# Cross-attention scores in three rounds of four key tiles, and products with the values of all heads once a batch, in a decoder layer

## The reference

```python
q = proj(hs, Wq, bq, S); k = proj(at, Wk, bk, T); v = proj(at, Wv, bv, T)
scores = jnp.einsum('bhsd,bhtd->bhst', q, k) / scale
scores = jnp.where(attend, jnp.clip(scores, -50.0, 50.0), -10000.0)
probs = jax.nn.softmax(jnp.clip(scores, -50.0, 50.0), axis=-1)
ctx = jnp.einsum('bhst,bhtd->bhsd', probs, v)
delta = rs * (ctx.transpose(0, 2, 1, 3).reshape(B, S, H) @ Wo.T + bo)
```

## Time and profile before

| | |
|---|---|
| runs | 1500.3 us median of 3 (1499.81 to 1503.2) |
| profiled execution | 1502.32 us; its span, first to last instruction, 1500.5 us |
| TensorE busy in the span | 1446.0 us, 96% |
| VectorE, ScalarE, GpSimd busy | 1051.9, 656.6, 579.7 us |
| mean granted TensorE clock | 0.986 |

### The profile page before, as it was taken

The page is one execution under the profiler, slowest core; times in us unless marked ns, Lnnn a source line. Parts: engine busy times, 40 slices in busy tenths (PEclk is TensorE's granted clock), DMA queues, the critical chain, the costliest instruction groups (busy, mean ns, idle before and its releaser), DMA issues. The chain is left out here.

```text
span 1500.5 us, 33618 instructions
## 1 busy us (share of the span) xinstructions
PE 1446.0 (96%) x13322; PEld 1125.9 (75%) x13322; DVE 1051.9 (70%) x2017; ACT 656.6 (44%) x861; POOL 579.7 (39%) x510
## 2 busy tenths in 40 slices
PE   7999999999899999999999999999999995998898
PEld 3688888887788888888888888888888884554333
DVE  2766655564577877777777777777777866677778
ACT  1333333333343433433334334333343432888986
POOL 0000000000244455444545454454545552752566
PEclk9999999999999999999999999999999997999999
DMA  6023333321511112111121121211212112357974
GB/s 217 29 78 102 102 102 101 102 81 45 182 40 61 52 45 72 45 47 64 45 72 44 41 71 45 72 39 45 72 45 70 41 56 64 81 171 285 355 260 154
DMA packets 80406, 138.58 MB, mean 92 GB/s; under 512 B 4882, under 2 KB 52498, under 8 KB 78562
## 3 DMA queue, kind: packets, MB, share of 16 engines
q1 hardware_dynamic: 80354, 137.87, 28.1%
HBM read 93.82 MB, written 44.04 MB: 92 GB/s over the span
## 5 line engine op out<-in xcount | busy, mean ns | idle before, releaser
L737 POOL TENSOR_TENSOR xa_psum<-xa_pr 125x448 f32<-125x448 f32 x126 | 153.9, 1221 | 236.0 <-DVE xa_pr L883 236.0
L883 DVE TENSOR_SCALAR xa_pr<-xa_pr,xa_keep 125x448 f32<-125x448 f32 x384 | 151.0, 450 | 108.1 <-ACT xa_pr L783 106.7
L783 ACT ACTIVATE xa_pr<-xa_bSC 125x1344 f32<-125x1344 f32 x128 | 165.6, 1294 | 138.1 <-PE xa_bSC L989 133.0
L764 ACT ACTIVATE xa_kf<-xa_bKV,xa_bk 128x376 f32<-128x376 f32 x128 | 73.8, 576 | 184.8 <-PE xa_bKV L913 184.8
L740 POOL TENSOR_TENSOR xa_psum<-xa_psum,xa_pr 125x448 f32<-125x448 f32 x126 | 147.3, 1169 | 12.1 <-POOL xa_psum L737 4.4
L913 PE MATMUL xa_bKV<-left_xn,wA 128*128 128x376 f32 x768 | 150.0, 344 | 0.0
L913 PE MATMUL xa_bKV<-xa_cx,wA 128*128 128x376 f32 x768 | 149.3, 343 | 0.0
L770 ACT COPY xa_v<-xa_bKV 125x512 f32<-125x512 f32 x96 | 56.3, 586 | 206.1 <-PE xa_bKV L924 200.9
L924 PE MATMUL xa_bKV<-wZ,left_xn 128*125 128x512 f32 x576 | 141.8, 394 | 1.7 <-POOL xa_ones L713 1.7
L924 PE MATMUL xa_bKV<-wZ,xa_cx 128*125 128x512 f32 x576 | 141.1, 393 | 0.0
L913 PEld LDWEIGHTS xa_bKV<-left_xn,wA 128*128 128x128 f32 x768 | 130.1, 188 | 8.9 <-issue 5.3
(11 more groups left out here) (192 smaller groups left out, 2560.3 us busy)
## 6 DMA issues: line engine op xcount, KB each, us to landing
wraw<-in_ctxT SPq DMA_DIRECT2D x32, 752.0 KB, 4.8
ff_hr<-h_scratch SPq DMA_DIRECT2D x7, 2048.0 KB, 11.1
wraw<-in_w SPq DMA_DIRECT2D x8, 1024.0 KB, 7.6
sa_raw<-in_x SPq DMA_DIRECT2D x8, 896.0 KB, 5.9
x_scratch<-left_qraw SPq DMA_DIRECT2D x8, 896.0 KB, 5.0
xa_qf<-q_scratch SPq DMA_DIRECT2D x32, 224.0 KB, 4.7
xa_x<-x_scratch SPq DMA_DIRECT2D x32, 224.0 KB, 4.7
x_scratch<-xa_x SPq DMA_DIRECT2D x32, 224.0 KB, 2.3
```

Source lines behind the costliest of these rows:

```text
L737: nc.gpsimd.tensor_tensor(psum01[:], third(h, 0), third(h, 1), ALU.add).then_inc(p01_ok, 1)
L764: nc.scalar.activation(kf[:, m, :], bKV[0][:, 0:TP], ACT.Identity, bias=bkt[:, m:m + 1]).then_inc(k_ok, 1)
L783: nc.scalar.activation(pr[h][:], bSC[0:TW, :, 0:TC * S], ACT.Exp, scale=XSCALE).then_inc(exp_ok, 1)
L883: nc.vector.tensor_scalar(third(h, t), third(h, t), EM50, bound, ALU.max, ALU.min).then_inc(pr_ok, 1)
```

## The change

The 12 tiles of scores of a batch (four heads of three) are counted through as units and computed in three rounds of four units (UR, NR), so that head 1 begins in round 0 and ends in round 1, and head 2 begins in round 1 and ends in round 2. pr has three buffers of four tiles in place of four of three, psum one buffer for each head and no psum01. TensorE's order in a batch becomes: scores round 0; attend of all four heads of the batch before, then sums of all four; keys 2, values 0 of the next batch; scores round 1, keys 3, values 1 of the next batch; scores round 2, keys 0 of the next batch, output of the batch before, keys 1 and values 2 of the next batch. The four products of a batch with their sums lie in the two banks bPV at once (pv_bank). tail2 and tail3 move one batch later, and so do the store of x2 and norm2. The last batch has an order of its own. The diff, cut:

```diff
--- before.py
+++ after.py
@@ -36,6 +36,8 @@
+UR = 4
+NR = C * TC // UR
@@ -637,8 +639,8 @@
-        pr = [n.sb(f"pr{i}", [TW, NJ, TC * S]) for i in range(C)]
-        psum01, psum = n.sb("psum01", [TW, NJ, S]), [n.sb(f"psum{i}", [TW, NJ, S]) for i in range(2)]
+        pr = [n.sb(f"pr{i}", [TW, NJ, UR * S]) for i in range(NR)]
+        psum = [n.sb(f"psum{h}", [TW, NJ, S]) for h in range(C)]
@@ -668,8 +670,27 @@
-        def third(h, t):
-            return pr[h][:, :, t * S:(t + 1) * S]
+        def early(b):
+            return isinstance(b, int) and b < 2
+        def tile_of(h, t):
+            u = h * TC + t
+            return pr[u // UR], u % UR * S
+        def part(h, t):
+            own, at_col = tile_of(h, t)
+            return own[:, :, at_col:at_col + S]
+        def units(r):
+            return [divmod(u, TC) for u in range(r * UR, (r + 1) * UR)]
+        def last_head(r):
+            return units(r)[-1][0]
+        def pv_bank(b, h):
+            if last(b):
+                return bPV[h][:, 0:2 * S] if h < 2 else bSC[:, h - 2, 0:2 * S]
+            return bPV[h % 2][:, h // 2 * 2 * S:(h // 2 + 1) * 2 * S]
@@ -692,19 +713,20 @@
-                    wait(sp, sc_done, 4 * b)
+                    wait(sp, sc_done, NR * b)
                     queries(b + 1, 1 - par)
+                if not early(b):
+                    sp.wait_ge(amax_ok, b - 1)
+                    sp.dma_start(x2_d[b - 2], x1[par][:]).then_inc(x2_out[par], 16)
                 wait(sp, x2_out[par], 8 * (b - par))
...
-                if not first(b):
-                    sp.wait_ge(amax_ok, b)
-                    sp.dma_start(x2_d[b - 1], x1[1 - par][:]).then_inc(x2_out[1 - par], 16)
@@ -727,21 +749,32 @@
+            def pair_sum(b, h):
+                pool.wait_ge(pr_ok, C * TC * b + TC * h + 2)
+                wait(pool, sum_done, C * (b - 1) + h + 1)
+                nc.gpsimd.tensor_tensor(psum[h][:], part(h, 0), part(h, 1), ALU.add).then_inc(p01_ok, 1)
+            def full_sum(b, h):
+                pool.wait_ge(pr_ok, C * TC * b + TC * h + 3)
+                pool.wait_ge(p01_ok, C * b + h + 1)
+                nc.gpsimd.tensor_tensor(psum[h][:], psum[h][:], part(h, 2), ALU.add).then_inc(ps_ok, 1)
...
+                if not early(b):
+                    norm2(b - 2)
+                pair_sum(b, 0)
+                full_sum(b, 0)
+                pair_sum(b, 1)
+                full_sum(b, 1)
+                if not first(b):
+                    x1_beta(b - 1, 1 - par)
+                if not last(b):
+                    pair_sum(b, 2)
+                    full_sum(b, 2)
+                    pair_sum(b, 3)
+                    full_sum(b, 3)
+                if not first(b):
+                    norm(b - 1)
@@ -772,25 +805,32 @@
+            keys(0, 1)
...
+            values(0, 0, 2)
+            def weights(b, r):
+                act.wait_ge(sc_done, NR * b + r + 1)
+                wait(act, pv_done, C * (b - 1) + last_head(r) + 1)
+                wait(act, ps_ok, C * (b - 1) + last_head(r) + 1)
+                nc.scalar.activation(pr[r][:], bSC[0:TW, :, 0:UR * S], ACT.Exp, scale=XSCALE).then_inc(exp_ok, 1)
...
+                weights(b, 0)
+                keys(b, 2)
+                if not last(b):
+                    values(b + 1, 1 - par, 0)
+                weights(b, 1)
+                keys(b, 3)
+                if not last(b):
+                    values(b + 1, 1 - par, 1)
+                weights(b, 2)
+                if not last(b):
+                    keys(b + 1, 0)
+                    if not (isinstance(b, int) and b >= B - 2):
...
+                    keys(b + 1, 1)
+                    values(b + 1, 1 - par, 2)
@@ -820,8 +860,8 @@
+                bank = pv_bank(b, h)
+                dve.wait_ge(sum_done, s + 1 if last(b) else C * b + C)
@@ -833,11 +873,11 @@
+            def tail1(b, mv=mv, st=st, bank=bKV[1]):
...
+                nc.vector.tensor_tensor(dl[:], bank[0:S, 0:D], bot[:], ALU.add).then_inc(dl_ok, 1)
@@ -871,35 +911,48 @@
+            def bounded(b, r):
+                dve.wait_ge(exp_ok, NR * b + r + 1)
+                for h, t in units(r):
+                    bound = keep[:, b * TC + t:b * TC + t + 1] if isinstance(b, int) else keep[:, bass.ds(b * TC + t, 1)]
+                    nc.vector.tensor_scalar(part(h, t), part(h, t), EM50, bound, ALU.max, ALU.min).then_inc(pr_ok, 1)
...
+                if not last(b):
+                    split_low(b + 1, 1 - par)
+                if not early(b):
+                    tail2(b - 2, par)
+                bounded(b, 0)
+                if not first(b):
+                    attended(b - 1, 0)
+                    attended(b - 1, 1)
+                if last(b):
+                    attended(b - 1, 2)
+                    attended(b - 1, 3)
+                bounded(b, 1)
+                if not first(b) and not last(b):
+                    attended(b - 1, 2)
+                    attended(b - 1, 3)
+                if not early(b):
+                    tail3(b - 2, par)
+                if first(b):
+                    for c in range(C):
+                        output_weights(c)
+                if last(b):
+                    tail1(b - 1)
+                    attended(b, 0)
+                    bounded(b, 2)
+                    attended(b, 1)
+                    return
+                bounded(b, 2)
+                if not first(b):
+                    tail1(b - 1)
...
+            attended(B - 1, 2)
+            attended(B - 1, 3)
...
+            tail1(B - 1, mv1, st1, bKV[0])
@@ -918,6 +971,7 @@
+                if t == 2:
@@ -926,18 +980,20 @@
+                bank = bKV[0] if last(b) else bKV[1]
+                if first(b):
+                    pe.wait_ge(wo_ok, 2 * C)
+                if last(b):
+                    pe.wait_ge(k_ok, 4 * B)
+                else:
+                    wait(pe, dl_ok, b)
+                    pe.wait_ge(v_ok, 3 * B if isinstance(b, int) and b == B - 2 else 3 * b + 8)
...
+                        mm = nc.tensor.matmul(bank[0:S, 0:D], cT[l][:, c, :], w["o"][r][:, c, :],
@@ -946,76 +1002,85 @@
+            keys(0, 0, 1)
+            values(0, 0, 2)
...
+                bank = pv_bank(b, h)
...
+                    wait(pe, cthi_ok, C * b)
+                pe.wait_ge(pr_ok, C * TC * b + TC * h + 3)
...
+                    own, col = tile_of(h, t)
...
+                bank = pv_bank(b, h)
...
+                        own, col = tile_of(h, t)
...
+                pe.wait_ge(ps_ok, C * b + h + 1)
...
+            def scores(b, par, r):
+                if r == 0:
+                    pe.wait_ge(q_in[par], 8 * (b - par) + 16)
+                pe.wait_ge(k_ok, 4 * b + last_head(r) + 1)
+                wait(pe, exp_ok, NR * b + r)
+                for i, (h, t) in enumerate(units(r)):
+                    for j in range(NJ):
+                        own = slice(j * HD, (j + 1) * HD)
+                        mm = nc.tensor.matmul(bSC[0:TW, j, i * S:(i + 1) * S], kf[own, h, t * TW:(t + 1) * TW], qf[par][own, h, :],
+                                              start=True, stop=True)
+                mm.then_inc(sc_done, 1)
...
+                scores(b, par, 0)
+                if not first(b):
+                    for h in range(C):
+                        attend(b - 1, 1 - par, h)
+                    for h in range(C):
+                        sums(b - 1, h)
+                keys(b, par, 2)
+                if not last(b):
+                    values(b + 1, 1 - par, 0)
+                scores(b, par, 1)
+                keys(b, par, 3)
+                if last(b):
+                    attend(b, par, 0)
+                    sums(b, 0)
+                    output(b - 1)
+                    scores(b, par, 2)
+                    attend(b, par, 1)
+                    sums(b, 1)
+                    return
+                values(b + 1, 1 - par, 1)
+                scores(b, par, 2)
+                keys(b + 1, 1 - par, 0)
+                if not first(b):
+                    output(b - 1)
+                keys(b + 1, 1 - par, 1)
+                values(b + 1, 1 - par, 2)
...
+            attend(B - 1, 1, 2)
+            sums(B - 1, 2)
...
+            attend(B - 1, 1, 3)
+            sums(B - 1, 3)
...

```

More of the change, by code:

```diff
@@ L834, in attended @@
                                                in1=cT[0][:, h, :].bitcast(F32), op0=ALU.add, op1=ALU.subtract).then_inc(ctlo_ok, 1)
-            def tail1(b, mv=mv, st=st):
+            def tail1(b, mv=mv, st=st, bank=bKV[1]):
                 if first(b):
@@ L872, in tail3 @@
                                         apply_absolute_value=True).then_inc(amax_ok, 1)
-            def body(b, par, pair):
-                for h in range(C):
-                    if h == 1 and not last(b):
-                        split_low(b + 1, 1 - par)
-                    if h == 3 and not first(b) and not last(b):
-                        tail2(b - 1, 1 - par)
```

(64 more changed lines are left out.)

58 lines of the change are left out of this document (5 added, 53 removed).

## The result

The changed kernel takes 1543.18 us (median of 4 runs, 1541.8 to 1545.68), the one before in the same runs 1500.14 (1499.81 to 1503.2): ratio 1.0289 (95% interval 1.0274 to 1.0304), 43 us slower. The forecast was 1510 with a range up to 1519. The direction came, and the wait that the prediction names; its size did not.

What follows compares the result with a forecast made beforehand. TensorE was taken to bound the cross-attention stage. Saved form changes -16, a later output wait +21 and both ends +5 gave +10 us on the 1500.3 median, so 1510 us, range 1487 to 1519.

Steps and rivals of the forecast that it cites:

- Scores: TensorE's score groups: three rounds at 3.23 us against four groups at 3.42, 0.19 saved a batch.
- A and Z: TensorE's products of heads with the values and their sums: four of each 3.22 us against 3.36, 0.14 saved.
- K after O: TensorE's keys chunk following the output product in the same form: 2.08 us instead of 2.17, 0.09 saved.
- O: TensorE's output product, now followed by keys instead of scores: 0.09 to 0.1 us saved a batch.
- V: TensorE's product for a tile of values, 2.89 us to the next scores; the output product has the same steps.
- change of form: TensorE switching weight shape between product groups: 10 a batch become 7, 0.18 us each.
- rival by which the saving doesn't come: First weight load costs, not the form change: 5 us saved; 1521 with the wait, 1500 without; no separate chance.
- S1: Start of TensorE's scores of round 1, from which both sides of the output wait are counted.
- two blocks: VectorE's attended pair held up by two GpSimd sums at the shared port: 5.1 to 5.6 us instead of 3.6.
- rival of a third block: Third VectorE hold-up, or tail1 and the next batch's bounding slip too: 1.7 us a batch, 1540; chance 0.08.
- one-block case: Only one VectorE hold-up before the output product, so its cT is in time: 1489 us; chance 0.27.
- The ends: Before batch 1's scores 2 us more, last batch 3 more (bounds 0 and 7): 5 us in all.

Runs made afterwards that it cites:

- heads early: Changed kernel with all four attended of the batch before run right after round 0's bounding, ahead of round 1's: 1495.53 us, ratio 0.996.
- both edits together: Changed kernel, head 1's pair sum waiting until all of round 1 is bounded, and x1_beta moved to the start of GpSimd's batch: 1497.38 us.
- all four cT free: Changed kernel, GpSimd's sums of head 1 and all behind them waiting until all four cT are done: 1501.76 us, ratio 1.0018.
- last-batch kernel: On heads early: in the last batch TensorE makes all sums, GpSimd none, and first products wait only for needed cT: 1489.8 us, ratio 0.9932.

## Why the prediction was right or wrong

**TensorE's savings: right.** 0.53 a batch was forecast and 0.54 came (26.96 to 26.42, shown with heads early). Not foreseen was the stop of 1.4 us in batch 2, once. Scores 3.21 for three rounds (3.23), A and Z 3.21 (3.22), K after O 2.06 (2.08), O 2.78 (0.11 less than V, 0.09 to 0.1). The larger figure for a change of form, from the rows, was the right one: three changes fewer gave 0.54, 0.18 each. The estimate of 0.16 a batch from the Trainium skill (TensorE: Matmul & The Clock Gate, Step-by-step) is less than a third of it. The rival by which the saving doesn't come has fallen.

**The place of the wait: right.** Output product, VectorE's last cT, 31 times. From S1 at 906.47 the output could start at 9.37 (913.67 + 2.17); forecast 9.4. The exponential starts 1.34 after S1 and takes 1.67 (1.34 and 1.65), and the bounding starts at 3.04, by the prediction's terms at 3.10.

**The size of the wait: wrong, and this is the step that failed.** The prediction put it: "Bounding follows after 0.05 to 0.15 and takes 0.363 a piece (907.66 to 908.75 for three): 1.45 for four." It took 3.26. The rate was read in a kernel whose sums wait for the last piece of their head, so those rows show no sum beside a piece, and the new release conditions were not followed piece by piece: head 1's pair sum needs one piece of the round, and its full sum the next. The prediction did go through orders in which the engines take turns, but with the first sum held up under the whole bounding, where in fact it got in between. Counted from S1:

| | forecast | came |
|---|---|---|
| bounding starts | 3.10 | 3.04 |
| first reciprocal | 4.55 | 6.30 |
| pair of attended | 5.1 to 5.6 (two blocks) | 4.52 (one block) |
| last cT | 9.65 to 10.15 | 10.82 |
| output starts | 9.4 to 10.2, taken 10.0 | 10.97 |

So one block of the attended was counted too many, two of the bounding were not counted, and the signal of the last cT takes 0.15 to TensorE, which was left out. With the 0.07 at the first weight load (2.85 for O against 2.78) that is 1.6 a batch where 0.7 stood: 48 us over 30 batches in place of 21. The rival of a third block was priced at 1.7 and 1540 us, and it is the one that came; it had a chance of 0.08. The one-block case, the rival on the faster side, is what both edits together made: 1497, where it had 1489. The stage's two ends took 8.2 there (5 in the forecast), the stop in batch 2 took 1.5, and its first V came 1.4 later than before.

The bounding being open to this stands in the Trainium skill too (SBUF — State Buffer, Who interferes with whom): it counts tensor_scalar among the operations that can, with suitable operands, take the shared ports as a pair, and then contend with GpSimd. The trace agrees (a piece of 1.34 for 0.45 beside a sum); the prediction weighed that section for the attended only.

**The ends: first right, last too small.** Up to batch 1's scores 2.3 us more (forecast 2). The last batch 6.8 more, at the upper bound of 0 to 7, where 3 was taken. VectorE works almost without a gap from 1265.75 to 1291.1 there and so sets the pace: four attended in a row (7.0 us) keep the bounding of round 1 back, GpSimd's sums hold up three pieces of the bounding in the first two rounds, and TensorE waits 2.79 for the bank and 4.69 for the bounding of round 2. The prediction counted two attended more, at 1.8 each, and no block. It also left out that TensorE can come back at the lower clock after a wait: 2.6 us for one stretch, of which at most 1.27 reached the end. The run without GpSimd's sums in that batch, where the clock stayed up and the waits were shorter, gave back 3.0.

**The sum.** By span: -2.9 + 2.3 + 33.5 + 6.8 + 0.8 = 40.5. Of the 33.5, -16.2 is the saving (30 x 0.54), 48.3 the wait (30 x 1.61) and 1.4 the stop in batch 2.

What stays open: what makes TensorE stop in batch 2, and why it doesn't with all four cT free. The edits that removed the blocks also moved when GpSimd's sums are ready, and TensorE's sums never became late in any of them, so how near that limit lies was not tried. Part of the distance between the medians of the last-batch kernel and the heads-early one isn't explained by their traces.

## What to carry to other kernels

When a change alters what a signal counts (here: which pieces release a sum), follow each release piece by piece before taking a duration from the old trace; a duration measured where nothing could run beside it is a lower bound. When an operation gets into the queue between a producer and the engine that sets the time, put it by its due time: the four attended were worth 1.6 us a batch, and no cT was late once they went ahead of the bounding of round 1, whose result TensorE takes only in the next batch. And where two engines contend, ask who waits for the loser: with heads early a piece of the bounding takes 719 ns in the mean, 681 in the slow kernel, and yet the time is 48 us shorter.

## What the runs showed of the hardware

- **Turns between VectorE and GpSimd.** A released sum gets in between two queued VectorE operations, and every further one too: two pieces at 1.34 in a row, each behind one sum. But not always. GpSimd's full sum, behind tail1's scalar_tensor_tensor and split_low (both inputs in SBUF), had to let both pass (heads early; VectorE's row, then GpSimd's):

```profile
896.45 1.71 DVE L841 TENSOR_TENSOR left_xn<-wraw,left_xn 128x1504 fp32r<-128x1504 f32 x1
```

```profile
896.06 3.10 POOL L760 TENSOR_TENSOR xa_psum<-xa_psum,xa_pr 125x448 f32<-125x448 f32 x1
```

The sum began at 896.06, while tail1's operation still ran, and lasted 3.10, up to 1.0 past split_low's end at 898.16. What decides between the two is open.
- **The clock.** In the changed kernel TensorE stood still for 4.7 us, and the granted clock was 0.50 for the 5.4 us behind it. After 2.79 us of standing still it stayed at 1.00 in the changed kernel and fell to 0.50 with heads early (24 records in 0.78 and in 1.29); after 2.72 it stayed at 1.00 in the last-batch kernel. So the length of the stop alone doesn't decide it.
- **Forms.** Seven changes between A and Z inside one form, in place of one, cost nothing measurable (3.20 against 3.21); a change between forms cost 0.18 (0.54 for three).
